# Second attention written in one fixed pattern on TensorE, ScalarE, VectorE and GpSimd

## The reference

```
x = x + first_attention(norm(x), ctx)    # one head
x = x + slots(norm(x))                   # 64 slots, top 8 per row, one gated update
x = x + second_attention(norm(x), ctx)   # 16 heads of 16, and its feed-forward:
                                         # relu(o W1 + b1) W2 + b2
x = x + experts(norm(x))                 # 8 experts, 2 picked per row
```

## Time and profile before

| | us |
|---|---|
| median of 3 runs | 552.11 |
| lowest, highest | 551.76, 552.84 |
| span of the profiled execution | 551.1 |
| busy in it: PE, DVE, ACT, POOL | 538.4, 284.0, 254.1, 168.7 |
| second attention, about | 183 to 320 |
| expert tiles, about | 334 to 545 |

### The profile page before, as it was taken

How to read it: one execution, slowest core, us unless ns; L and a number is a source line. 1 busy time by engine, 2 the same in 40 slices (tenths; PEclk the granted TensorE clock), 3 DMA queues, 4 the chain that set the end, 5 groups by cost and what they waited for, 6 DMA issues and landing times.

```text
span 551.1 us, 11061 instructions
## 1 busy us (share of the span) xinstructions
PE 538.4 (98%) x3967; PEld 444.4 (81%) x3968; DVE 284.0 (52%) x847; ACT 254.1 (46%) x587; POOL 168.7 (31%) x152
## 2 busy tenths in 40 slices
PE   9999999999999999999999889999999999999995
PEld 7887878777655676777777679999999999999995
DVE  4867676988562776855788865722212111212110
ACT  1343476263346767687787834542222222222221
POOL 2211000002145222332222043354335454445533
PEclk9999999999999999999999999999999999999999
DMA  8940000000110000300470657968788888898733
GB/s 320 403 141 1 2 0 2 0 1 2 38 39 0 2 2 1 116 1 2 135 287 7 227 172 244 318 187 268 221 246 219 248 229 236 239 255 238 239 66 38
DMA packets 28651, 74.30 MB, mean 135 GB/s; under 512 B 5600, under 2 KB 20320, under 8 KB 23360
## 3 DMA queue, kind: packets, MB, share of 16 engines
q1 hardware_dynamic: 18592, 61.87, 31.9%
q0 software_dynamic: 7488, 10.39, 10.6%
q10 hardware_dynamic: 2528, 1.48, 0.9%
HBM read 62.88 MB, written 10.85 MB: 134 GB/s over the span
## 4 chain that ended last, share of the span: by engine, by line
PE 93%; ACT 4%; DVE 1%; issue 1%; POOL 0%; DVEq 0%; POOLq 0%
PE ps L897 64%; PE ps L1193 12%; PE ps L901 11%; ACT ring L617 2%; PE ps L1041 1%; PE ps L1050 1%; ACT ring L624 1%; PE ps L1053 1%; PE ps L1044 1%; PE ps L981 1%; PE ps L1024 1%; ACT HF L629 0%; ACT ring L658 0%; POOL out_x L422 0%; PE ps L1122 0%
## 5 line engine op out<-in xcount | busy, mean ns | idle before, releaser
L897 PE MATMUL ps<-keep,arena 128*128 128x128 f32 (+2 forms) x976 | 114.9, 274 | 0.0
L897 PEld LDWEIGHTS ps<-keep,arena 128*128 128x128 f32 x976 | 112.8, 192 | 1.5 <-issue 1.1
L2014 DVE TENSOR_TENSOR keep<-keep,ps 128x512 f32<-128x512 f32 x39 | 26.8, 686 | 145.7 <-PE ps L897 124.2
L422 POOL DMA_INDIRECT out_x<-arena,row_no x38 | 59.9, 1576 | 102.1 <-DMA out_x<-arena,row_no 65.2
L1193 PE MATMUL ps<-arena,keep 128*128 x312 | 73.7, 380 | 0.1
L665 ACT COPY keep<-ps 128x256 f32<-128x256 f32 x39 | 14.5, 372 | 107.1 <-PE ps L901 103.8
L381 POOL TENSOR_TENSOR ring<-arena,keep 128x512 f32<-128x512 f32 x32 | 33.5, 1049 | 96.9 <-PE ps L897 79.8
L1193 PEld LDWEIGHTS ps<-arena,keep 128*128 128x128 f32 x312 | 56.4, 190 | 6.6 <-issue 0.3
L617 ACT ACTIVATE ring<-ps,mx 128x128 f32<-128x128 f32 x192 | 52.3, 403 | 6.2 <-DVE mx L1714 6.2
L897 PE MATMUL ps<-ring,arena 128*32 128x128 f32 (+1 forms) x640 | 53.1, 348 | 1.5 <-ACT ring L624 1.4
L373 POOL TENSOR_TENSOR var_x<-var_x,minus_half 128x4 f32<-128x4 f32 x16 | 16.5, 1036 | 115.8 <-DVE var_x L1570 115.8
(11 more groups left out here) (266 smaller groups left out, 816.2 us busy)
## 6 DMA issues: line engine op xcount, KB each, us to landing
arena<-in_w SPq DMA_DIRECT2D x29, 1024.0 KB
w_first<-in_w SPq DMA_DIRECT2D x10, 1024.0 KB
arena<-in_w SPq DMA_DIRECT2D x8, 512.0 KB, 7.3
keep<-in_keep SPq DMA_DIRECT2D x1, 3115.0 KB, 20.8
ring<-in_fold SPq DMA_DIRECT2D x1, 2112.0 KB, 12.7
arena<-in_x SPq DMA_DIRECT2D x4, 512.0 KB, 10.5
arena<-in_ctxT SPq DMA_DIRECT2D x4, 512.0 KB, 7.1
arena<-in_ctx SPq DMA_DIRECT2D x4, 384.0 KB, 11.2
```

Of the source, the lines that this page charges most:

```text
L422: pool.indirect_dma_start(out=out_d, out_offset=bass.IndirectOffsetOnAxis(ap=rows_at, axis=0), in_=YO[t % DEEP], in_offset=None, compute_o ...
L897: ins = pe.matmul(out, w, m, start=(k == 0), stop=(k == len(pairs) - 1))
L2014: dve.tensor_tensor(HA[r % 2], HA[r % 2], ps[:, 2 * (r % 2) + 1, :], ALU.mult).then_inc(act_ok, 1)
```

## The change

No call is added or removed, and no call's content is altered, but for the constant COUNT_AT, which goes from 13 to 12. The lists of calls of second attention are rewritten into one pattern that repeats for each batch: two scores, two attention steps of the batch before, then hidden layer, turn, outputs and turn for the feed-forward of the batch before that. ScalarE has two exponentials, the relu, and two copies in its pattern; VectorE two shifts, a division, and a sum. The count of the early picks is read before hidden1(12) instead of hidden1(13), and the routing calls on VectorE stand earlier against the batches. On GpSimd the roots of groups 0 and 2 go ahead of spread_keys(14) and spread_keys(30).

```diff
-COUNT_AT = 13
+COUNT_AT = 12
...
             spread_keys(13)
+            root(0, "xh4")
             spread_keys(14)
-            root(0, "xh4")
...
             exp1(3)
             probs1_turned(2)
+            exp1(4)
             probs1_turned(3)
-            exp1(4)
+            exp1(5)
             hidden1(0)
             probs1_turned(4)
-            exp1(5)
+            probs1_turned(5)
             exp1(6)
-            probs1_turned(5)
+            exp1(7)
             hidden1(1)
...
             attend1(6)
             attend1(7)
+            hidden1(2)
             turn_probs1(8)
-            hidden1(2)
+            outputs1(2)
+            turn_probs1(9)
             score1(10)
-            turn_probs1(9)
-            outputs1(2)
             score1(11)
             attend1(8)
             attend1(9)
...
             turn_x4(0)
+            hidden1(5)
+            turn_probs1(14)
             outputs1(5)
-            turn_probs1(14)
+            turn_probs1(15)
             score1(16)
+            score1(17)
+            attend1(14)
+            attend1(15)
             gate_logits(0)
-            attend1(14)
-            turn_probs1(15)
+            turn_probs1(16)
             hidden1(6)
...
             shift(7)
-            shift(8)
             divide(2)
             add_outputs(1)
+            shift(8)
             shift(9)
```

More of the change, by code:

```diff
@@ L486, in _ @@
             spread_keys(29)
+            root(2, "xh4")
             spread_keys(30)
-            root(2, "xh4")
             spread_keys(31)
@@ L1407, in _ @@
             attend1(9)
+            hidden1(3)
             turn_probs1(10)
-            hidden1(3)
+            outputs1(3)
+            turn_probs1(11)
             score1(12)
-            turn_probs1(11)
-            outputs1(3)
             score1(13)
@@ L1468, in _ @@
             attend1(23)
+            gate_logits(1)
             turn_probs1(24)
+            hidden1(10)
+            turn_probs1(25)
+            outputs1(10)
             score1(26)
-            outputs1(10)
+            score1(27)
             attend1(24)
-            turn_probs1(25)
+            attend1(25)
             hidden1(11)
-            score1(27)
-            attend1(25)
+            turn_probs1(26)
             outputs1(11)
-            turn_probs1(26)
+            turn_probs1(27)
             score1(28)
-            hidden1(12)
-            turn_probs1(27)
             score1(29)
-            outputs1(12)
             attend1(26)
@@ L1487, in _ @@
             turn_probs1(28)
+            hidden1(12)
+            turn_probs1(29)
+            outputs1(12)
             score1(30)
-            turn_probs1(29)
-            hidden1(13)
+            score1(31)
             attend1(28)
             attend1(29)
-            score1(31)
             turn_x4(2)
+            hidden1(13)
+            turn_probs1(30)
             outputs1(13)
-            turn_probs1(30)
-            gate_logits(2)
-            attend1(30)
-            hidden1(14)
             turn_probs1(31)
             place_early()
+            gate_logits(2)
+            hidden1(14)
+            attend1(30)
             attend1(31)
@@ L2232, in _ @@
             shift(22)
-            norm_x4(1)
             shift(23)
@@ L2236, in _ @@
             add_outputs(9)
+            shift(24)
+            shift(25)
             gate_logits(1)
+            divide(11)
             route_shift(0, EB)
-            shift(24)
             route_groups(0, EB)
-            shift(25)
-            divide(11)
+            add_outputs(10)
             shift(26)
-            add_outputs(10)
+            shift(27)
             route_compare(0, EB)
+            divide(12)
             route_ties(0, EB)
-            shift(27)
-            divide(12)
+            route_ranks(0, EB)
             add_outputs(11)
+            gather_stats(2, "xh4")
             shift(28)
-            route_ranks(0, EB)
+            shift(29)
             route_weights(0, EB)
-            gather_stats(2, "xh4")
-            shift(29)
-            add_outputs(12)
-            divide(13)
-            early_counts()
-            early_ranks()
-            norm_x4(2)
-            early_columns(0)
+            early_counts()
+            divide(13)
+            early_ranks()
+            early_columns(0)
+            norm_x4(2)
+            add_outputs(12)
             shift(30)
+            shift(31)
             early_tiles()
             divide(14)
-            add_outputs(13)
-            shift(31)
-            gate_logits(2)
             early_places()
             early_hot()
+            add_outputs(13)
             early_rows()
+            gate_logits(2)
             divide(15)
```

108 lines of the change are left out of this document (51 added, 57 removed).

## The result

| | us |
|---|---|
| changed kernel, median of 4 runs | 580.54 (579.57 to 582.81) |
| before, median of 4 runs beside it | 551.93 (551.71 to 552.84) |
| ratio after to before, with its interval | 1.0519 (1.0492 to 1.0546) |
| span of the profiled execution, before and after | 551.1 and 578.8 |
| forecast | 570.5 (565 to 575) |

The change makes the kernel 5.2% slower. The direction and the larger part of the loss were forecast; the time lies 5.5 us above the upper end of the range. The first look at the page after is again the chain that ended last. TensorE holds 66% of it instead of 93%, and ScalarE, VectorE and transfers have come in.

What follows compares the result with a forecast made beforehand. The prediction took TensorE to bound the kernel. Late batches 12.7, early batches 4.9, first batch 3.7, last batches 0.3, less 3.2 recovered, gave +18.4 us on 552.1: 570.5 us, range 565 to 575.

Steps and rivals of the forecast that it cites:

- The walk of the waits: Second attention: step-by-step timing of the new queues, giving TensorE's waits for ScalarE in each batch.
- Late batches: Batches 6 to 13: outputs wait for the relu behind two eight-piece exponentials, 1.7 us in five; 12.7 us over all eight.
- the three with the turn ahead: Batches 6, 10, 12: the turn waits 1.0 us for exp(2b+4), the relu costs another 0.4; 1.4 us each.
- Early batches: Batches 1 to 5: outputs wait for the relu, 1.07 us in b = 1 to 4, 0.6 in b = 5; together 4.9 us.
- Batch 14: Last batches of second attention: the relu follows copy(31), adding 0.3 us.
- First batch: Start of the pattern: attention(3) waits for copy(3) behind exp(4), 3.7 us; net term also 3.7 us.
- 0.85 us less: First batch: possible reduction if VectorE's division product and GpSimd's key spreading miss each other; not taken.
- Recovered waits: Stretch 305:320: all 3.2 us that TensorE lost in the old order taken off the sum.
- the clock: Rival, 6%: the first batch's pause lowers TensorE's granted clock once, costing 2.7 us, time 573.2; shorter waits harmless.
- behind 334 us nothing changes: Expert tiles, 334 to 540 us: TensorE is busy for 205.93 of 206 us, so earlier losses pass through one for one.
- half of it: Rival, 8%: only late batches pay, the early pair hides; 565.6 us.
- No slower: Rival, 5%: the pattern keeps TensorE fed and ScalarE keeps up; 552.7 or 548.5 us.

Runs made afterwards that it cites:

- the copy first: Changed kernel with one ScalarE swap taken back, the copy of unit 3 ahead of exp(4) again: 572.52 us, ratio 1.0369.
- the count a batch later: Changed kernel with COUNT_AT back at 13, its VectorE steps and the hot columns on ScalarE moved later: 577.98 us, ratio 1.0462.
- the repeat: Changed kernel, unaltered, run and profiled a second time: 574.81 us, ratio 1.0403.
- the first profile: Profile of the changed kernel, unaltered, in its first set of runs: median 580.54 us, ratio 1.0519.
- kernel before with the swap: Kernel before with exp(4) put ahead of the copy of unit 3 on ScalarE, nothing else: 558.14 us, ratio 1.0100.
- one exponential: Changed kernel with BIAS_FROM 32 instead of 16, so odd late units are shifted on VectorE and exponentiated in one piece: 576.68 us, ratio 1.0461.
- the third profile: Profile of the changed kernel, unaltered, in its third set of runs: median 579.39 us, ratio 1.0497.

## Why the forecast was wrong

**The walk of the waits was right.** Late batches: 1.90 to 1.95 us in five (forecast 1.7); 1.40, 1.40 and 1.52 in the three with the turn ahead (1.4), of which 1.23 to 1.34 is the first turn's wait (1.0) and only 0.17 or 0.18 the rest (0.4). Early batches: 1.15 in four (1.07), 0.83 in b = 5 (0.6). Batch 14: 0.22 (0.3). First batch: 3.55 (3.7). Most were too small by up to 0.25; together 23.1 us of waits where the terms had 21.6. Without falls the first down step comes 17.4 us later than before (351.47 against 334.11), and the profile of before was 1.0 us late already when score(5) began (184.15 against 183.12), so 18.4 us from there on, exactly the sum. The medians say 18.0. That it is exact is luck: the waits were 1.5 us larger than their terms, and what came back was larger by as much. So a time of 570 was a fair price for waits alone, and 0.85 us less was rightly not taken: the division's product ran beside GpSimd's key spreading again (1.28 us at 182.26, the spreading at 182.22). The Trainium skill (SBUF — State Buffer, SBUF: two separate sides) has the shared port pair as an exclusive lock between such a product and a GpSimd instruction; that row agrees.

**Recovered waits:** the forecast took all of 3.2 us off as gone with the old order. In the new one the stretch 305:320 loses 3.24 us again, but these are the waits that the walk had counted (1.90 and 1.34), so the step holds. By the sums above it was even too small: 23.1 - 18.4 = 4.7 us came back. Where the other 1.5 us lie isn't assigned.

**The step that failed is the clock.** The sum of 570.5 has no term for it; in the profile after it measured 6.3 us (four falls), and in the other runs of this kernel it is two to about six falls. The forecast had it as a rival at 6%, with one fall of 2.7 us in the first batch and "the 1 to 1.7 us waits are harmless". The fall in the first batch came in all eight profiles that have its pause of 3.5 us. And the five waits of 1.90 to 1.96 us are not harmless: in the four profiles of the changed kernel and in that with the copy first, 9 of 25 were followed by a fall. None of the pauses of 1.35 us or less was in these profiles. (With the count a batch later it is one of four more.) The forecast argued from 305:320 of the kernel before, where the sum of the pauses is 3.2 us at a clock of 1.00; but no single one is over 1.06 us there. What should have been compared is the length of one pause: 1.7 us is longer than any pause of the kernel before in this part, so its trace said nothing about it. The price of one fall was too high (2.7, read from the 32 passes at the kernel's start, against 1.6, with 2.7 only for the long ones), the number too low: two to four in the profiles. I had leaned on the rule of the Trainium skill about long pauses (TensorE: Matmul & The Clock Gate, HAM oscillation — how this bites in real kernels); the section behind it on the same page (A second HAM failure mode: psum-queue depth-cycling) names the other case, a TensorE that pauses briefly but often between groups and whose clock goes back and forth. The trace agrees in part: waits shorter than the one in the first batch were followed by falls, but only those of 1.9 us, and the waits of 1.15 us that come every 9.8 us never were.

**The other terms that were missing.** The late division cost 3.0 us in the profile after, besides the fall behind its pause. The forecast said too that behind 334 us nothing changes, since TensorE is busy for 205.93 of 206 us. It is busy for 205.12 of 206 now; the expert tiles took 1.2 us more, 0.8 of it for a late fetch. The late end of the result transfers, 4.7 us, is in one profile of four, and not in the one that was forecast, which ends 6.3 us behind the last matmuls as before (6.4). The clock alone would do for the miss: 580.5 - 6.3 = 574.2 us lies in the range. The 574.81 of the repeat lies in it too, but only because the range was wide: it has three falls.

**What stays open.** Why the division of batch 15 was released 3.3 us late in the first profile and not in the other three isn't known; no experiment was made on it. The first four runs have a surplus of 2 to 3 us in span times clock over the other sets, so it, or something of its size, was in all of them; but only one was profiled, and the chip of that set isn't on record. Why the result transfers fell behind in one run isn't known either, nor why the falls are more in some runs. The chip isn't told apart from the set. Even the kernel before has two runs of 33 beside the experiments, at 554.21 and 556.24 us, with a mean clock of 0.995 where the others have 0.997 to 1.000; they weren't profiled.

The other rivals: "half of it", by which the early batches hide, is out, since they wait 1.15 us each. "No slower" is out. The chances of slower against faster were right.

## What to carry to other kernels

A pause of TensorE is priced at its length plus, where it is longer than what the trace shows to be harmless, a possible fall of the clock; look up in the trace which single pauses stayed at full clock, not their sum, and treat everything longer as open. Whether a wait or a fall costs the time can be told by filling the pause with matmuls whose result nobody uses. In a fixed pattern of several engines the instruction that the bound engine needs first has to stand first on its helper: two exponentials ahead of one relu made waits of 1.15 to 1.95 us in most batches, though ScalarE had time to spare.

## What the runs showed of the hardware that was not expected

The same pause of 1.90 to 1.96 us was followed by a clock of 0.50 in some executions and 1.00 in others. Most stretches at 0.50 cost 1.6 us; three of them, two behind the pause of 3.55 us in the first batch and one behind a pause of 2.03 us, were about twice as long (kernel before with the swap, the count later, one exponential), and the one that was compared cost 2.7 us. A chain of transfers in which each waits for the landing of the one before went at 5.3 to 5.7 us a piece (475.97 to 492.50 in the third profile) while the weights were being read and a fetch stood between each two, and at 4.5 us at the end, without either. Which of the two makes the difference was not tested.
